# A Swin transformer block on one core: the order of its preparation, with weights loaded as two groups on two queues

## The chip, the core and the metric

The kernel runs on one core of a Trainium2 chip, all data in 32-bit floats. The metric is the device time of one execution in microseconds (us), the median of several runs.

## What is computed

The input x is 32 images of 56 x 56 positions with 128 channels, and the block is one shifted-window attention layer followed by a feed-forward layer:

```
h    = layernorm(x) * g1 + b1, rolled by (-3, -3), cut into 7 x 7 windows (49 tokens)
q,k,v = split(h @ w_qkv + b_qkv), 4 heads of 32 channels
attn = softmax(q k^T / sqrt(32) + rel_bias[head] + mask(-100 across a border))
x    = x + rolled back(attn v @ w_proj + b_proj)
out  = x + gelu((layernorm(x)*g2 + b2) @ w_fc1 + b_fc1) @ w_fc2 + b_fc2
```

## The kernel before, in words

The work is cut into **steps** of 14 image rows (two bands of 7 rows, 784 tokens), four to an image, 128 in all. A step's tokens lie as 7 tiles of 112 tokens x 128 channels. The instruction streams of the five engines are written out in full, without loops on the chip; `run_steps` (L61) calls each engine's `step(n)` for n from -3 to 129, and one `step(n)` holds pieces of several steps of data at once: statistics for step n+3 (VectorE, L638), normalising, transposing and the q product of step n+2, scores and attention of n+1, projection and the first layer of the feed-forward part of n, and so on. So the first three calls (n = -3, -2, -1) fill the pipeline. The order on each engine is fixed by hand, and semaphores join the engines.

**The start (the preparation).** SyncE issues the six transfers of the first step's tokens (`load(0, 0)`, L269), then thirteen transfers of weights, vectors and the mask (L270 to L277), all of which count up one semaphore, `weights_loaded`; then half of the relative-position table (`load_rel`, L254, seven transfers) and the tokens of steps 1 to 3. ScalarE's queue issues the other half of that table (L348). VectorE fills tiles with zeros (L482 to L490; the last is `psum`), waits for all thirteen transfers (L491), and folds the layernorm gains into the weights: `wqk`, `wv`, `wfc1` (L493 to L496). It splits `wqk` and `wfc1` into a rounded part `_hi` and a remainder `_lo` (L499 to L503), for products made as three passes in a faster format (`product`, L720).

TensorE waits for the same thirteen transfers (L667) and multiplies the weights by the layernorm offsets, three one-column products from `w_qkv` (L669) and four from `w_fc1` (L672). VectorE makes the biases from them (L508 to L512) and a widened copy of the v bias (L515), with which TensorE makes one more product (L676). From that VectorE makes `brow_proj` (L517), the row that is added to the tokens ahead of the projection's result. GpSimd waits for `weights_loaded` and `brow_ready` (L308, L309) before its first step, ScalarE for `weights_ready` and `bias_v_ready`.

**The first steps.** Only then do the steps begin. VectorE: `stats1(k)` (seven `bn_stats`, L532) and `mean_var` (six short operations, L539 to L548) for step 0, in call n = -3; the same for step 1, then `normalise` of step 0 (seven operations, L553), in call n = -2; statistics of step 2, `split_x` (L594, the remainder of band 1 of the transposed tokens) and `normalise` of step 1 in call n = -1; and in call 0 first `make_bias_rel` (four additions, L525: relative-position bias plus mask), then the scores of step 0 (L568 and on). GpSimd makes 1/sqrt(variance) with one power operation a step (`power`, L318) and adds `brow_proj` to the tokens (`add_row`, L321). TensorE transposes the seven normalised tiles (L695), ScalarE copies them out of PSUM (`copy_x`, L379) and rounds band 1 (L384). TensorE then makes q and k of band 0 (L728), q of band 1 when the split is there (L721 to L723), and the scores (L688).

Of the kernel before, what the change touches and what calls it, by code (L numbers as in the profile page):

```python
# [10 lines left out]
ALU = mybir.AluOpType  # L11
# [4 lines left out]
C = 128  # L16
# [31 lines left out]
def swin_block(nc, x, g1, b1, w_qkv, b_qkv, w_proj, b_proj, rel_slices, g2, b2, w_fc1, b_fc1, w_fc2,  # L48
# [4 lines left out]
    def has(k):  # L53

        return 0 <= k < steps

# [8 lines left out]
    with ExitStack() as ctx:  # L65
# [75 lines left out]
        weights_loaded = sem("weights_loaded")  # L141
# [7 lines left out]
        bias_v_ready = sem("bias_v_ready")  # L149
        brow_product = sem("brow_product")  # L150
# [109 lines left out]
        def _(sp):  # L260
# [9 lines left out]
            for dst, src in ((wqkv[:, :], w_qkv), (vecs[:, 0:1], g1), (vecs[:, 1:2], b1), (vecs[:, 2:3], g2),  # L270
                             (vecs[:, 3:4], b2), (bqkv[:, :], b_qkv), (wproj[:, :], w_proj),
                             (wfc1_raw[:, :], w_fc1), (bfc1[:, :], b_fc1),
                             (wfc2[:, :, :], w_fc2.rearrange("(k p) n -> p k n", p=C)),
                             (brow_proj_in[:, :], b_proj.to_broadcast([TOK, C])),
                             (brow_fc2[:, :], b_fc2.to_broadcast([TOK, C])),
                             (mask_sb[:, :, :, :], mask)):
                sp.dma_start(dst, src).then_inc(weights_loaded, 16)  # L277
# [23 lines left out]
        def _(pool):  # L301
# [6 lines left out]
            pool.wait_ge(weights_loaded, 13 * 16)  # L308
            pool.wait_ge(brow_ready, 1)  # L309
# [14 lines left out]
            def step(n):  # L324
# [16 lines left out]
                if has(n - 1):  # L341
                    wait(pool, var2_ready, upto(n - 1))
                    power(rstd2, ve2, rstd2_ready)
            run_steps(step)

        @block.scalar
        def _(act):
            load_rel(act, 1)  # L348
# [61 lines left out]
            def load_gelu_table():  # L410
                act.activation(table_probe[:, :], bias_h[:, 0:1], ACT.Gelu).then_inc(gelu_loaded, 1)
# [69 lines left out]
        def _(dve):  # L481
# [9 lines left out]
            dve.wait_ge(weights_loaded, 13 * 16)  # L491

            dve.tensor_scalar(wqk[:, 0, :], wqkv[:, 0:C], vecs[:, 0:1], SCALE, ALU.mult, ALU.mult)  # L493
            dve.tensor_scalar(wqk[:, 1, :], wqkv[:, C:2 * C], vecs[:, 0:1], None, ALU.mult)
            dve.tensor_scalar(wv[:, :], wqkv[:, 2 * C:3 * C], vecs[:, 0:1], None, ALU.mult)
            dve.tensor_scalar(wfc1[:, :], wfc1_raw[:, :], vecs[:, 2:3], None, ALU.mult).then_inc(weights_scaled, 1)  # L496

            dve.wait_ge(weights_scaled, 1)
            dve.tensor_copy(wqk_hi[:, :, :], wqk[:, :, :])  # L499
            dve.tensor_copy(wfc1_hi[:, :], wfc1[:, :]).then_inc(weights_scaled, 1)  # L500
            dve.wait_ge(weights_scaled, 2)
            dve.tensor_tensor(wqk_lo[:, :, :], wqk[:, :, :], wqk_hi[:, :, :], ALU.subtract)
            dve.tensor_tensor(wfc1_lo[:, :], wfc1[:, :], wfc1_hi[:, :], ALU.subtract).then_inc(weights_ready, 1)  # L503

            dve.wait_ge(bias_products, 1)
            made = psum[:, QKVO_BANK, :]
            for parity in range(2):
                dve.tensor_scalar(bias_q[:, parity:parity + 1], made[:, 0:1], bqkv[:, 0:1],  # L508
                                  parity_scale[:, parity:parity + 1], ALU.add, ALU.mult)
            dve.tensor_tensor(bias_k[:, :], made[:, 1:2], bqkv[:, 1:2], ALU.add)  # L510
            dve.tensor_tensor(bias_v[:, :], made[:, 2:3], bqkv[:, 2:3], ALU.add)
# [408 lines left out]
```

## Time and profile before

| | us |
|---|---|
| median of 3 runs | 3122.12 |
| lowest and highest run | 3111.51 and 3128.21 |
| profiled execution, own time | 3099.51 |
| its span, first to last instruction | 3097.7 |

In the profile, a row of the timeline gives the start, the duration, the engine, the source line, the operation with the tile written and the tiles read, the number of instructions merged into the row, and in brackets how long the engine had stood idle and what released it. PE is TensorE's matmul, PEld its weight load, DVE VectorE, ACT ScalarE, POOL GpSimd, SP SyncE; SPq and ACTq are the instructions by which a queue issues transfers. Over the whole span PE is busy for 97%, VectorE for 90%, ScalarE for 74% and GpSimd for 42%.

### The profile page before, as it was taken

Reading aid. Unit: us, or ns where it says so; the run is one execution under the profiler, and the core shown is the slowest. Engines: PE = TensorE matmul, PEld = TensorE weight load, DVE = VectorE, ACT = ScalarE, POOL = GpSimd, SP = SyncE. Lnnn points to the kernel's source line nnn. Section 1 sums busy time; section 2 is a strip of 40 time slices with the busy share of each in tenths; the row PEclk is TensorE's granted clock in tenths of the full one; section 3 lists DMA queues with packets and bytes.
Section 4 is the critical chain, followed back from the end, with each engine's and each line's share of the span. In section 5 each row is a group of like instructions: output and inputs, shape, how many; then the busy total and the mean of one; then the engine's idle time right before and its main releaser. Section 6 shows DMA issues by size and latency. Waiting matters only on the chain.

```text
span 3097.7 us, 119627 instructions
## 1 busy us (share of the span) xinstructions
PE 3003.0 (97%) x51984; PEld 2725.4 (88%) x51984; DVE 2803.2 (90%) x7463; ACT 2305.0 (74%) x4482; POOL 1306.6 (42%) x775
## 2 busy tenths in 40 slices
PE   5999999999999999999999999999999999999998
PEld 3898888989988898998899889988999888998897
DVE  7899988999989899999999999989999899999994
ACT  4777777777777777777777777777777777777774
POOL 2444444444434444444444444444444344444442
PEclk8999999999999999999999999999999999999999
DMA  1111111111111111111111111111111111111100
GB/s 55 34 34 34 44 34 34 33 44 34 34 33 44 34 34 35 43 34 33 44 33 34 40 37 34 36 41 34 34 39 39 33 34 39 39 33 37 41 18 22
DMA packets 217572, 111.81 MB, mean 36 GB/s; under 512 B 15094, under 2 KB 216790, under 8 KB 217046
## 3 DMA queue, kind: packets, MB, share of 16 engines
q1 hardware_dynamic: 216899, 104.14, 13.2%
q8 instruction: 408, 6.68, 0.9%
q14 instruction: 118, 0.97, 0.1%
q10 hardware_dynamic: 147, 0.02, 0.0%
HBM read 52.73 MB, written 51.38 MB: 34 GB/s over the span
## 4 chain that ended last, share of the span: by engine, by line
PE 59%; DVE 38%; issue 2%; ACT 0%; SPq 0%; DMA 0%; POOL 0%; POOLq 0%; ACTq 0%; DVEq 0%
PE psum L721 11%; DVE xn L553 9%; PE psum L722 7%; PE psum L723 7%; PE psum L688 7%; DVE row_sum L580 7%; PE psum L742 7%; PE psum L749 6%; PE psum L716 6%; DVE stream L587 4%; DVE scores L568 4%; DVE row_max L571 4%; DVE scores L573 4%; PE psum L703 4%; PE psum L695 3%; DVE x2T_lo L598 2%
## 5 line engine op out<-in xcount | busy, mean ns | idle before, releaser
L763 PEld LDWEIGHTS psum<-wfc,hT 128*112 128x112 f32 x7168 | 806.1, 177 | 39.2 <-issue 21.5
L763 PE MATMUL psum<-wfc,hT 128*112 128x128 f32 x7168 | 824.1, 273 | 1.5 <-ACT hT L407 1.5
L407 ACT ACTIVATE hT<-psum,bias_h 128x392 f32<-128x392 f32 x1024 | 578.8, 594 | 314.6 <-PE psum L723 301.7
L318 POOL TENSOR_TENSOR rstd<-ve,minus_half 112x7 f32<-112x7 f32 x256 | 381.1, 1489 | 986.7 <-DVE ve L548 986.7
L314 POOL TENSOR_TENSOR probs<-probs,row_inv 128x784 f32<-128x784 f32 x256 | 388.7, 1519 | 689.8 <-DVE row_inv L582 689.8
L553 DVE TENSOR_SCALAR xn<-stream,mean,rstd 112x128 f32<-112x128 f32 x896 | 460.4, 571 | 1.6 <-POOL rstd L318 1.6
L587 DVE TENSOR_TENSOR stream<-psum,stream 112x512 f32<-112x512 f32 (+1 forms) x512 | 305.6, 606 | 169.7 <-PE psum L749 153.0
L721 PE MATMUL psum<-x2T_hi,wfc_hi 128*128 128x392 f32 x1024 | 405.0, 395 | 9.2 <-DVE x2T_lo L598 2.0
L722 PE MATMUL psum<-x2T_hi,wfc_lo 128*128 128x392 f32 x1024 | 351.9, 344 | 12.4 <-issue 12.4
L723 PE MATMUL psum<-x2T_lo,wfc_hi 128*128 128x392 f32 x1024 | 351.9, 344 | 0.0
L394 ACT ACTIVATE qd<-psum,bias_q,parity_one 128x392 f32<-128x392 f32 x512 | 316.9, 669 | 3.3 <-PE psum L723 3.3
L321 POOL TENSOR_TENSOR stream<-stream,brow_fc 112x896 f32<-112x896 f32 x128 | 269.0, 2102 | 93.5 <-DVE xn L553 93.5
L721 PEld LDWEIGHTS psum<-x2T_hi,wfc_hi 128*128 128x128 f32 x1024 | 193.5, 189 | 106.5 <-DVE x2T_lo L598 87.4
L695 PE MATMUL psum<-ident,xn 112*128 112x112 f32 x1792 | 271.3, 268 | 10.6 <-DVE xn L553 9.1
L568 DVE TENSOR_TENSOR scores<-psum,bias_rel 128x784 f32<-128x784 f32 x256 | 247.2, 966 | 34.3 <-PE psum L688 34.2
L321 POOL TENSOR_TENSOR stream<-x_in,brow_proj 112x896 f32<-112x896 f32 x128 | 270.3, 2112 | 0.5 <-DMA out<-stream 0.5
L742 PE MATMUL psum<-wv,xT 128*113 128x128 f32 x2048 | 265.4, 272 | 0.0
L573 DVE TENSOR_TENSOR scores<-scores,row_max 128x784 f32<-128x784 f32 x256 | 249.5, 975 | 8.7
L571 DVE TENSOR_REDUCE row_max<-scores 128x16 f32<-128x784 f32 x256 | 248.3, 970 | 8.8
L353 ACT ACTIVATE probs<-scores 128x784 f32<-128x784 f32 x256 | 223.7, 874 | 42.5 <-DVE scores L573 41.1
L361 ACT ACTIVATE probsT<-psum 128x452 f32<-128x452 f32 x512 | 252.0, 550 | 0.6 <-PE psum L703 0.6
L389 ACT ACTIVATE x2T_hi<-psum 128x448 fp32r<-128x448 f32 (+1 forms) x256 | 127.5, 498 | 166.7 <-PE psum L695 166.6
(78 smaller groups left out, 5663.2 us busy)
## 6 DMA issues: line engine op xcount, KB each, us to landing
x_in<-in_x SPq DMA_DIRECT2D x224, 168.0 KB
out<-stream SPq DMA_DIRECT2D x224, 168.0 KB
x_in<-in_x SPq DMA_DIRECT2D x224, 17.5 KB
out<-stream SPq DMA_DIRECT2D x224, 17.5 KB
x_in<-in_x SPq DMA_DIRECT2D x224, 10.5 KB
out<-stream SPq DMA_DIRECT2D x224, 10.5 KB
x_in<-in_x SPq DMA_DIRECT2D x32, 96.0 KB
out<-stream SPq DMA_DIRECT2D x32, 96.0 KB
```

The costliest lines, as they stand in the source:

```text
L314: pool.tensor_tensor(p, p, r.unsqueeze(2).to_broadcast([128, 2 * WINDOWS, N]), ALU.mult).then_inc(probs_normed[band], 1)
L318: pool.tensor_tensor(rstd[:, :], ve[:, :], minus_half[:, :], ALU.pow).then_inc(ready, 1)
L321: pool.tensor_tensor(stream[:, k % STEPS, :, :], src[:, k % STEPS, :, :], row[:, :].unsqueeze(1).to_broadcast([TOK, TILES, C]), ALU.add).t ...
L407: act.activation(hT[:, chunk, band * BAND:(band + 1) * BAND], tok_psum(c)[:, 0:BAND], ACT.Gelu, bias=bias_h[:, chunk:chunk + 1]).then_inc( ...
L553: last = dve.tensor_scalar(dst[:, t, :], src[:, t, :], mean[:, t:t + 1], rstd[:, t:t + 1], ALU.subtract, ALU.mult)
L573: dve.tensor_tensor(rows, rows, mx.unsqueeze(2).to_broadcast([128, 2 * WINDOWS, N]), ALU.subtract).then_inc(scores_shifted[band], 1)
L587: dve.tensor_tensor(s, tok_psum(h)[0:TOK, 0:(t1 - t0) * C], s, ALU.add).then_inc(ready[h], 1)
L721: pe.matmul(made, w_hi, x_hi, start=True, stop=False)
L722: pe.matmul(made, w_lo, x_hi, start=False, stop=False)
L723: return pe.matmul(made, w_hi, x_lo, start=False, stop=True)
L742: last = pe.matmul(qkvo_psum(V_BANK[band])[0:rows, pair * C:(pair + 1) * C], windows[:, 0:rows], wv[:, :], start=True, stop=True)
L763: last = pe.matmul(tok_psum(h)[0:TOK, (t - t0) * C:(t - t0 + 1) * C], hT[:, chunk, t * TOK:(t + 1) * TOK], wfc2[:, chunk, :], start=chunk ...
```

## The change

The thirteen transfers become two groups. SyncE issues six (`front_loaded`): w_qkv, g1, b1, b_qkv, w_proj and b_proj. ScalarE's queue issues seven (`back_loaded`): g2, b2, w_fc1, b_fc1, w_fc2, b_fc2 and the mask, ahead of its half of the relative-position table. Statistics, power, normalising and transposing of step 0 move out of the step calls into the preparation: the statistics stand ahead of the wait for the front group, the normalising behind the scaling of `wqk` and `wv`, the transposes ahead of the wait for the back group. What belongs to `w_fc1` is prepared behind them. `fresh(k)` (0 < k < steps) takes the place of `has(k)` where step 0 has now been dealt with. TensorE waits for `weights_ready`, `bias_h_ready` and `brow_ready` before its first step call. GpSimd's power of step 0 stands ahead of its wait for the back group. The table-loading instruction of ScalarE reads `parity_one` in place of `bias_h`. No transfer and no arithmetic is added or removed.

```diff
+    def fresh(k):
+
+        return 0 < k < steps
...
 @block.sync
             load(0, 0)
-            for dst, src in ((wqkv[:, :], w_qkv), (vecs[:, 0:1], g1), (vecs[:, 1:2], b1), (vecs[:, 2:3], g2),
-                             (vecs[:, 3:4], b2), (bqkv[:, :], b_qkv), (wproj[:, :], w_proj),
...
-                sp.dma_start(dst, src).then_inc(weights_loaded, 16)
+            for dst, src in ((wqkv[:, :], w_qkv), (vecs[:, 0:1], g1), (vecs[:, 1:2], b1), (bqkv[:, :], b_qkv),
+                             (wproj[:, :], w_proj), (brow_proj_in[:, :], b_proj.to_broadcast([TOK, C]))):
+                sp.dma_start(dst, src).then_inc(front_loaded, 16)
             load_rel(sp, 0)
...
 @block.gpsimd
-            pool.wait_ge(weights_loaded, 13 * 16)
-            pool.wait_ge(brow_ready, 1)
...
-                if has(n + 2):
+                if fresh(n + 2):
                     wait(pool, var1_ready, upto(n + 2))
                     power(rstd1, ve1, rstd1_ready)
...
+            pool.wait_ge(var1_ready, 1)
+            power(rstd1, ve1, rstd1_ready)
+            pool.wait_ge(back_loaded, 7 * 16)
+            pool.wait_ge(brow_ready, 1)
             run_steps(step)
...
 @block.scalar
+            for dst, src in ((vecs[:, 2:3], g2), (vecs[:, 3:4], b2), (wfc1_raw[:, :], w_fc1), (bfc1[:, :], b_fc1),
+                             (wfc2[:, :, :], w_fc2.rearrange("(k p) n -> p k n", p=C)),
+                             (brow_fc2[:, :], b_fc2.to_broadcast([TOK, C])), (mask_sb[:, :, :, :], mask)):
+                act.dma_start(dst, src).then_inc(back_loaded, 16)
             load_rel(act, 1)
...
 @block.vector
-            dve.wait_ge(weights_loaded, 13 * 16)
...
+            dve.wait_ge(x_loaded[0], dma_count(0, 0))
+            stats1(0)
+            mean_var(raw1, part1, mean1, ve1, raw1_done, parts1_done, stats1_done, var1_ready, 1)
+
+            dve.wait_ge(front_loaded, 6 * 16)
+            dve.tensor_scalar(wqk[:, 0, :], wqkv[:, 0:C], vecs[:, 0:1], SCALE, ALU.mult, ALU.mult)
+            dve.tensor_scalar(wqk[:, 1, :], wqkv[:, C:2 * C], vecs[:, 0:1], None, ALU.mult)
+            dve.tensor_scalar(wv[:, :], wqkv[:, 2 * C:3 * C], vecs[:, 0:1], None, ALU.mult).then_inc(weights_scaled, 1)
+            dve.wait_ge(weights_scaled, 1)
+            dve.tensor_copy(wqk_hi[:, :, :], wqk[:, :, :]).then_inc(weights_scaled, 1)
+
+            dve.wait_ge(rstd1_ready, 1)
+            for h in range(2):
+                normalise(xn1, x_in[:, 0, :, :], mean1, rstd1, xn1_ready, h)
+
+            dve.wait_ge(weights_scaled, 2)
+            dve.tensor_tensor(wqk_lo[:, :, :], wqk[:, :, :], wqk_hi[:, :, :], ALU.subtract)
+            dve.wait_ge(bias_products, 1)
...
+            dve.wait_ge(back_loaded, 7 * 16)
+            dve.tensor_scalar(wfc1[:, :], wfc1_raw[:, :], vecs[:, 2:3], None, ALU.mult).then_inc(weights_scaled, 1)
+            dve.wait_ge(weights_scaled, 3)
+            dve.tensor_copy(wfc1_hi[:, :], wfc1[:, :]).then_inc(weights_scaled, 1)
+            dve.wait_ge(weights_scaled, 4)
+            dve.tensor_tensor(wfc1_lo[:, :], wfc1[:, :], wfc1_hi[:, :], ALU.subtract).then_inc(weights_ready, 1)
+            dve.wait_ge(bias_products, 2)
+            dve.tensor_tensor(bias_h[:, :], psum[:, QKVO_BANK + 1, 0:CHUNKS], bfc1[:, :], ALU.add).then_inc(bias_h_ready, 1)
+            dve.wait_ge(brow_product, 1)
+            dve.tensor_tensor(brow_proj[:, :], psum[0:TOK, QKVO_BANK, 0:C], brow_proj_in[:, :],
+                              ALU.add).then_inc(brow_ready, 1)
...
 @block.tensor
+            pe.wait_ge(front_loaded, 6 * 16)
+            for k in range(3):
+                last = pe.matmul(psum[:, QKVO_BANK, k:k + 1], wqkv[:, k * C:(k + 1) * C], vecs[:, 1:2],
+                                 start=True, stop=True)
+            last.then_inc(bias_products, 1)
+            pe.wait_ge(ident_ready, 1)
+            for h in range(2):
+                pe.wait_ge(xn1_ready[h], 1)
+                transpose_tiles(xn1, h, xT_made)
+            pe.wait_ge(back_loaded, 7 * 16)
+            for k in range(CHUNKS):
+                last = pe.matmul(psum[:, QKVO_BANK + 1, k:k + 1], wfc1_raw[:, k * C:(k + 1) * C], vecs[:, 3:4],
+                                 start=True, stop=True)
+            last.then_inc(bias_products, 1)
+            pe.wait_ge(bias_v_ready, 2)
+            pe.matmul(psum[0:TOK, QKVO_BANK, 0:C], bias_v_wide[:, :], wproj[:, :], start=True,
+                      stop=True).then_inc(brow_product, 1)
+            pe.wait_ge(weights_ready, 2)
+            pe.wait_ge(bias_h_ready, 1)
+            pe.wait_ge(brow_ready, 1)
```

## Rows read from the trace of the kernel before

**Rows 1.** The page: busy time of each engine.

```profile
PE 3003.0 (97%) x51984; PEld 2725.4 (88%) x51984; DVE 2803.2 (90%) x7463; ACT 2305.0 (74%) x4482; POOL 1306.6 (42%) x775
```

**Rows 2.** The timeline of SyncE's queue: each step's stores, from step 1 on.

```profile
118.05 2.26 SPq L267 DMA_DIRECT2D out<-stream  x6
...
141.33 2.26 SPq L267 DMA_DIRECT2D out<-stream  x6
...
167.46 3.35 SPq L267 DMA_DIRECT2D out<-stream  x9
...
2934.79 2.26 SPq L267 DMA_DIRECT2D out<-stream  x6
```

**Rows 3.** The waits of PE between 141 and 167 us (total, times, longest).

```profile
PE psum L716 <- issue: 2.6, 1, 2.6
```

**Rows 4.** The chain of waits in the first 120 us (start, duration, what).

```profile
8.71 4.91 DMA mask_sb<-in_mask
```

**Rows 5.** The timeline of SyncE's queue at the start.

```profile
0.74 2.20 SPq L263 DMA_DIRECT2D x_in<-in_x  x6
2.98 0.36 SPq L277 DMA_DIRECT2D wqkv<-in_w_qkv  x1
...
11.60 48.33 SPq L263 DMA_DIRECT2D x_in<-in_x  x39
```

**Rows 6.** The timeline of the engines during the preparation.

```profile
6.17 1.76 DVE L490 MEMSET psum<- 128x2048 f32 x1 [0.42 <-issue]
...
13.65 0.29 DVE L493 TENSOR_SCALAR wqk<-wqkv,vecs 128x128 f32<-128x128 f32 x1 [5.71 <-DMA mask_sb<-in_mask]
...
14.97 1.85 PE L672 MATMUL psum<-vecs,wfc_raw 128*128 128x1 f32 x8
...
15.76 0.68 DVE L503 TENSOR_TENSOR wfc_lo<-wfc,wfc_hi 128x512 fp32r<-128x512 f32 x1
...
17.82 0.77 PE L676 MATMUL psum<-wproj,bias_v_wide 128*112 128x128 f32 x2 [1.01 <-DVE bias_v_wide L515]
```

**Rows 7.** The same timeline, first steps: what the change moves, and what follows it.

```profile
18.84 1.44 DVE L532 BATCH_NORM_STATS2 raw<-x_in 112x6 f32<-112x128 f32 x7
...
21.37 1.49 POOL L318 TENSOR_TENSOR rstd<-ve,minus_half 112x7 f32<-112x7 f32 x1 [19.85 <-DVE ve L548]
22.90 1.89 DVE L553 TENSOR_SCALAR xn<-x_in,mean,rstd 112x128 f32<-112x128 f32 x7 [0.34 <-POOL rstd L318]
24.16 1.54 PE L695 MATMUL psum<-ident,xn 112*128 112x112 f32 x7 [5.57 <-DVE xn L553]
...
25.25 1.28 ACT L379 ACT_TABLE_LOAD   x1 [25.25 <-PE psum L695]
...
27.03 2.07 POOL L321 TENSOR_TENSOR stream<-x_in,brow_proj 112x896 f32<-112x896 f32 x1
...
27.62 2.98 PE L728 MATMUL psum<-xT,wqk 128*128 128x392 f32 x4 [1.92 <-ACT xT L379]
...
32.97 3.89 DVE L525 TENSOR_TENSOR bias_rel<-mask_sb,rel 128x392 f32<-128x392 f32 x4 [0.94 <-PE psum L688]
...
33.58 2.39 POOL L321 TENSOR_TENSOR stream<-x_in,brow_proj 112x896 f32<-112x896 f32 x1
```

**Rows 8.** Transfers of the first 70 us (KB, median us from issue to landing).

```profile
brow_proj_in<-in_b_proj SPq DMA_DIRECT2D x1, 56.0 KB, 3.7
```

**Rows 9.** Busy time by stretch: PE, PEld, DVE, ACT, POOL, then PEclk, DMA share, GB/s.

```profile
2.00:4.00 2.00, 0.00 (x0) 0.00 (x0) 1.62 (x2) 0.00 (x0) 0.00 (x0) 1.00 0.69 181
6.00:8.00 2.00, 0.00 (x0) 0.00 (x0) 1.76 (x1) 0.00 (x0) 0.00 (x0) 1.00 0.29 66
```

**Rows 10.** By tile or line: duration in ns as min/median/max, first and last start.

```profile
L525 DVE TENSOR_TENSOR bias_rel<-mask_sb,rel x4: 554/564/2453, 33.0 to 36.3; 128x392 f32<-128x392 f32 x4
...
L594 DVE TENSOR_TENSOR xT_lo<-xT,xT_hi x12: 556/556/1367, 28.2 to 289.9; 128x392 fp32r<-128x392 f32 x12
...
L553 DVE TENSOR_SCALAR xn<-stream,mean,rstd x4: 254/338/1589, 65.8 to 67.7; 112x128 f32<-112x128 f32 x4
```

More of the change, by code:

```diff
@@ L490, in _ @@
             dve.memset(psum[:, 0:4, :], 0.0).then_inc(weights_ready, 1)
-            dve.wait_ge(weights_loaded, 13 * 16)
[L493 to L511, printed above, removed]
-            dve.tensor_tensor(bias_h[:, :], made[:, 3:3 + CHUNKS], bfc1[:, :], ALU.add).then_inc(bias_v_ready, 1)
-            dve.wait_ge(bias_v_ready, 1)
-            dve.tensor_copy(bias_v_wide[:, :], bias_v[:, 0:1].to_broadcast([C, TOK])).then_inc(bias_v_ready, 1)
-            dve.wait_ge(brow_product, 1)
-            dve.tensor_tensor(brow_proj[:, :], psum[0:TOK, QKVO_BANK + 1, 0:C], brow_proj_in[:, :],
-                              ALU.add).then_inc(brow_ready, 1)
             def make_bias_rel():
                 dve.wait_ge(rel_loaded, 2 * WIN * 16)
+                dve.wait_ge(back_loaded, 7 * 16)
                 for last_band in range(2):
@@ new lines, in _ @@
+            dve.wait_ge(bias_products, 1)
+            made = psum[:, QKVO_BANK, :]
+            for parity in range(2):
+                dve.tensor_scalar(bias_q[:, parity:parity + 1], made[:, 0:1], bqkv[:, 0:1],
+                                  parity_scale[:, parity:parity + 1], ALU.add, ALU.mult)
+            dve.tensor_tensor(bias_k[:, :], made[:, 1:2], bqkv[:, 1:2], ALU.add)
+            dve.tensor_tensor(bias_v[:, :], made[:, 2:3], bqkv[:, 2:3], ALU.add).then_inc(bias_v_ready, 1)
+            dve.wait_ge(bias_v_ready, 1)
@@ L650, in step @@
                     split_x(n + 1, 1)
-                if has(n + 2):
+                if fresh(n + 2):
                     if n < 0:
@@ L655, in step @@
                     normalise(xn1, x_in[:, (n + 2) % STEPS, :, :], mean1, rstd1, xn1_ready, 1)
-                if has(n + 3):
+                if fresh(n + 3):
                     wait(dve, raw1_done, upto(n + 3))
@@ L665, in _ @@
         def _(pe):
-            pe.wait_ge(weights_loaded, 13 * 16)
-            for k in range(3):
-                pe.matmul(psum[:, QKVO_BANK, k:k + 1], wqkv[:, k * C:(k + 1) * C], vecs[:, 1:2],
-                          start=True, stop=True)
-            for k in range(CHUNKS):
-                last = pe.matmul(psum[:, QKVO_BANK, 3 + k:4 + k], wfc1_raw[:, k * C:(k + 1) * C], vecs[:, 3:4],
-                                 start=True, stop=True)
-            last.then_inc(bias_products, 1)
-            pe.wait_ge(bias_v_ready, 2)
-            pe.matmul(psum[0:TOK, QKVO_BANK + 1, 0:C], bias_v_wide[:, :], wproj[:, :], start=True,
-                      stop=True).then_inc(brow_product, 1)
-            pe.wait_ge(weights_ready, 2)
-            pe.wait_ge(ident_ready, 1)
             def make_scores(band):
@@ L797, in step @@
                     make_values(n + 1, 0)
-                if has(n + 2):
+                if fresh(n + 2):
                     wait(pe, gelu_done[4], upto(n - 1))
@@ L808, in step @@
                     make_scores(1)
-                if has(n + 2):
+                if fresh(n + 2):
                     wait(pe, gelu_done[3], upto(n - 1))
```

15 lines of the change are left out of this document (7 added, 8 removed).

## Prediction

> **What bounds the kernel now.** I began with the page: PE is busy for 97% of the span, VectorE for 90% [rows 1]. Busy shares are averages, so next the rhythm of the steps, read from SyncE's queue: consecutive stores start 23.28 us apart (141.33 - 118.05), and then once 26.13 us apart (167.46 - 141.33) [rows 2]. The ordinary step is TensorE's own length; in the long one PE stood for 2.6 us on "issue", that is with no other engine to wait for, in the middle of the small attention products of L716 [rows 3]. The change edits none of this. Its 128 steps come behind a start that it does edit, so I read the start as an offset: whatever the start gives, every later step is earlier by as much, as long as the filling of the pipeline is bound by a chain that begins there.
>
> The chain of waits of the first 120 us names that start: the mask, issued at 8.71 us, lands 4.91 us later and is the last of the thirteen transfers to arrive [rows 4]. SyncE issues one after another: tokens from 0.74, the first weight at 2.98, the tokens of steps 1 to 3 from 11.60, behind the mask [rows 5]. VectorE has finished its zero filling at 7.93 (6.17 + 1.76) and idles 5.71 us until 13.65 [rows 6]. Behind that lies a serial stretch: scaling, bias products and `brow_proj`, statistics of step 0 at 18.84, its power at 21.37, its seven normalising operations at 22.90, its transposes at 24.16 [rows 7]. The place to compare the two kernels is the end of `make_bias_rel`, 36.86 us (32.97 + 3.89) [rows 7]: behind it stands only VectorE's own work on the scores, which neither kernel can start sooner.
>
> **The change, step by step.** I lay the new order out with the old durations.
>
> 1. *Tokens of step 0.* VectorE may start their statistics at 7.93. From statistics to power takes 2.53 us (18.84 to 21.37), from power to normalising 1.53 (to 22.90), the seven operations 1.89 [rows 7]. So: power at 10.5, normalising 12.0 to 13.9. The transposes begin 1.26 us behind the first normalising operation (24.16 - 22.90) and take 1.54: 13.3 to 14.8. The scaling of `wqk`, `wv` and the rounding, some 1.0 us by the starts around L493, fit under the power's 1.5 us and cost nothing, if the front group has landed by about 11; without that cover they cost their own 1.0.
>
> 2. *The front group.* The issue of its last member moves forward: five issues at 0.47 us behind the one at 2.98 make 5.4. (0.47 is the spacing of the thirteen: 8.71 - 2.98 = 5.73 over twelve.) The slowest small one of its kind, `brow_proj_in`, took 3.7 us to land [rows 8]: 9.1. That leaves about 2 us of room before it is wanted.
>
> 3. *The back group.* Seven issues at 0.47 from about 0.8 put the mask at 3.6 and its landing, by its own 4.91, at 8.5. Both groups then want the transfer engines at once. The engines had room: 69% and 181 GB/s at 2 to 4 us, but 29% and 66 GB/s at 6 to 8, when SyncE was issuing small vectors [rows 9]. Tokens of step 0 and all thirteen are about 1.7 MB; at 181 GB/s from 2 us on that ends at 11.4. The group is first wanted by PE at 14.8. Nothing waits if it lands by then. At the worst, the engines do no better than the old start's mean, in which SyncE's pace was part: 1.7 MB from 2 to 13.6, 147 GB/s [rows 4]. SyncE now issues the tokens of steps 1 and 2 (0.8 MB) from 8.3 on, so these may all be carried as well before the group's last byte: 2.5 MB at 147 GB/s end at 19. I take 11.4, from the row of a stretch in which transfers were waiting, and keep 19 for the range.
>
> The Trainium skill (DMA: Bandwidth & Descriptors, "Issuing engines are not separate DMA queues") says that transfers started from several engines run on the same 16 DMA engines and interleave, and that one saves only the issuing time. By this the groups would land together, no later than the bytes allow, and the start keeps the sum below; the same rule says that tokens of step 0 can be held up by the back group, which is a rival below.
>
> 4. *Behind the transposes.* PE: four products with `w_fc1`, 1.85 us [rows 6], 14.8 to 16.7; then the product for `brow_proj`, from whose start to that of the statistics behind it pass 1.02 us (17.82 to 18.84) [rows 6, 7]. So statistics of step 1 start at 17.7. VectorE's work beside that ends sooner: behind 13.9 come `wqk_lo` and the biases (1.3 by the old starts), then scaling, rounding and remainder of `wfc1`, some 1.7 with its last piece 0.68 [rows 6]: 16.9. Here PE is the later by less than 1 us. ScalarE, released with the biases at 15.0, loads its table (1.28) [rows 7] and copies step 0 out by 17.3; before, this stood in the chain behind the transposes, now it is hidden beside the `w_fc1` work. GpSimd's and TensorE's waits for the back group hold nothing that is wanted earlier.
>
> 5. *The filling.* Statistics of step 1 at 17.7, its power 2.53 later at 20.2 to 21.7; statistics of step 2 (1.44) at 20.2 to 21.6. `split_x` no longer waits for ScalarE and runs 21.6 to 22.1 at its median of 0.56 [rows 10]. Before, it took 1.37, because GpSimd's `add_row` (27.03 to 29.10) [rows 7] was running. The same `add_row` now starts right behind the power, at 21.7, and falls on normalising of step 1. What this does is shown in a row of a later stage: under a long GpSimd operation one of four normalising operations takes 1589 ns where the others take 254 to 338 [rows 10]. So the first is held until about 23.9, and the seven end near 25.7. Of what was won on the split, 1.7 us go back. `mean_var` of step 2 (0.7) ends at 26.5, and `make_bias_rel` starts there. PE is not what it waits for: q and k take 2.98 from 17.9 [rows 7], q of band 1 starts behind the split at 22.1, and the scores follow about 2 us on.
>
> 6. *`make_bias_rel`.* Four at 0.56 [rows 10] from 26.5. GpSimd: power 26.5 to 28.0, `add_row` 28.0 to 30.1. Three pass, the fourth (28.2) is held until 30.1, as one was before (2453 ns against 564), and ends at 30.7.
>
> **The sum:** 36.86 - 30.7 = 6.2 us. The median of the runs is 3122.12, so I forecast **3115.9 us**. The profiled execution took 3099.51, 22.6 us less than that median and less than the lowest run shown; its successor should have a span near 3097.7 - 6.2 = 3091.5 if it were as lucky. That one gap is more than three times the gain. About 0.5% (15.6 us) is what a measurement here can tell from no change.
>
> Bounds of the gain: above, 9.7 us, the move of the first q product (27.62 to 17.9) [rows 7] if nothing collides. Below, 1.9: the back group at 19.1 holds PE up by 4.3 us (14.8 to 19.1), and 6.2 becomes 1.9.
>
> **The rivals.**
>
> *The gain is held whole.* GpSimd's `add_row` slips between VectorE's work and all of it goes through: up to 9.7 us, 3112.4. For it: VectorE's order against GpSimd's is decided here by tenths. Against: twice in the old start, and in the row of a later stage, one was held.
>
> *The wait comes back as another.* Sharing delays the tokens of step 0, the front or the back group until 15 us or later. The gain is 0 to 3, the time 3119 to 3122. For it: both queues ask at once for what one spread over 8.7 us, and the mask alone took 4.91 [rows 4]. Against: the engines' 29% share while SyncE issued small vectors [rows 9].
>
> *Slower: the pauses of PE move.* About every fifth gap between stores is longer than 23.3 us, some 27 from the one at 167.46 to the one at 2934.79 [rows 2]. The one at 167.46 is 2.85 us over, with PE's pause on L716 in it [rows 3]. The change puts some three more waits into PE's stream ahead of the first step, which moves the place of every later pause. If five more of the 27 fell on L716, at 2.8 us each instead of an estimated 0.5 elsewhere, 11.5 us are added, 6.2 are won, and the time is 3127. It decides from three on (6.9 against 6.2). Against: three instructions are little beside the some 400 matmuls of a step, of which L716 has 128, so at most one pause should change its place.
>
> *The change doesn't do what it says.* If the code order on VectorE let the front group's wait come first, step 0 would gain nothing; the diff shows statistics ahead of it, so I hold this at nothing and count it under the second rival.
>
> **How the numbers follow.** The forecast's case (a gain of 3 to 8): 0.65. The whole gain: 0.12. The wait comes back: 0.15. PE's pauses, or anything else that makes it slower: 0.08. None but a part of the last can by itself reach 15.6 us; what can is the scatter of the runs, 16.7 us from lowest to highest and 28.7 with the profiled one. Around a gain of 6, a difference of medians with a spread of some 8 us passes 15.6 about one time in eight, and the whole gain adds a little: faster 0.16, slower 0.04, same 0.80. The range: down to 3101, the whole gain and 11 us of scatter (3122.12 - 3111.51); up to 3128, the slower rival, which is also the highest run.
>
> **What would show it.** In the changed kernel's profile: statistics of step 0 within 0.5 us of 7.9; normalising from 12.0; VectorE's wait for the front group under the power; PE's `w_fc1` products right behind the transposes with no transfer as releaser; the first q product near 18; the first normalising operation of step 1 near 2 us long; the end of `make_bias_rel` near 30.7; stores 23.3 us apart as before, the first one 6 us sooner. I am wrong if PE or VectorE stands on a transfer at 11 to 15 us, if the lead at `make_bias_rel` is not there at the first store, or if the pauses at L716 become more.

## The result and the profile after

| | before | after |
|---|---|---|
| median of 11 runs, us | 3117.28 | 3131.86 |
| lowest and highest, us | 3101.30, 3128.21 | 3125.10, 3143.53 |
| profiled execution, own time, us | 3099.51 | 3132.80 |
| its span, us | 3097.7 | 3131.1 |

The ratio of the times is **1.0054** with a 95% interval of 1.0031 to 1.0077: the changed kernel is slower, by about 17 us (the means of the runs; the medians differ by 14.6), a small change but one that the interval keeps apart from none. Its median of 3131.86 lies above the predicted range. Yet its start went as planned, and better. The timeline of the changed kernel's start, to hold against [rows 6] and [rows 7]:

```profile
7.85 1.39 DVE L511 BATCH_NORM_STATS2 raw<-x_in 112x6 f32<-112x128 f32 x7
...
11.06 0.29 DVE L585 TENSOR_SCALAR wqk<-wqkv,vecs 128x128 f32<-128x128 f32 x1 [0.99 <-DMA brow_proj_in<-in_b_proj]
...
11.98 1.88 DVE L532 TENSOR_SCALAR xn<-x_in,mean,rstd 112x128 f32<-112x128 f32 x7
...
13.24 1.54 PE L699 MATMUL psum<-ident,xn 112*128 112x112 f32 x7 [0.72 <-DVE xn L532]
...
14.57 1.73 PE L783 MATMUL psum<-vecs,wfc_raw 128*128 128x1 f32 x8
...
17.16 1.44 DVE L511 BATCH_NORM_STATS2 raw<-x_in 112x6 f32<-112x128 f32 x7
...
17.50 2.95 PE L732 MATMUL psum<-xT,wqk 128*128 128x392 f32 x4 [0.58 <-DVE brow_proj L616]
...
21.14 2.15 POOL L320 TENSOR_TENSOR stream<-x_in,brow_proj 112x896 f32<-112x896 f32 x1
21.26 3.65 DVE L532 TENSOR_SCALAR xn<-x_in,mean,rstd 112x128 f32<-112x128 f32 x7
...
25.57 2.00 DVE L504 TENSOR_TENSOR bias_rel<-mask_sb,rel 128x392 f32<-128x392 f32 x4
```

`make_bias_rel` ends at 27.57 instead of 36.86 us, 9.3 us sooner. In these two traces the lead is still whole at the first store. SyncE's queue, kernel before:

```profile
94.75 2.27 SPq L267 DMA_DIRECT2D out<-stream  x6
```

and the changed kernel:

```profile
85.45 2.28 SPq L273 DMA_DIRECT2D out<-stream  x6
...
108.75 2.25 SPq L273 DMA_DIRECT2D out<-stream  x6
```

94.75 - 85.45 = 9.3 us, and the next step again takes 23.30. What costs comes later and a little at a time. I took the 121 gaps between consecutive stores in each trace and added up what each has over 23.3 us: 44.5 us in the kernel before, 86.0 in the changed one, 41.5 more. With the start (-9.3) and the last stretch (+1.5, from the last of those stores to the end) that is, to within 0.3 us, the 33.4 us between the two spans. The waits of PE say what the long gaps are made of; "issue" is time in which PE waits for no other engine and no transfer of data. Kernel before (total, times, longest):

```profile
PE psum L716 <- issue: 19.2, 9, 3.0
...
PE psum L722 <- issue: 12.4, 8, 1.7
...
PE psum L749 <- issue: 1.8, 6, 0.4
```

Changed kernel:

```profile
PE psum L720 <- issue: 37.1, 16, 3.0
PE psum L725 <- issue: 14.8, 8, 2.3
...
PE psum L753 <- issue: 4.0, 8, 0.9
```

L716 and L720 are the same code, the small products of the attention, 128 matmul records a step. TensorE paused there 16 times instead of 9. **One such pause, step by step.** The same step of both kernels, PE's timeline of the kernel before:

```profile
788.70 1.37 PE L716 MATMUL psum<-probsT,vs 49*32 49x49 f32 x128
```

and of the changed kernel:

```profile
780.50 1.25 PE L720 MATMUL psum<-probsT,vs 49*32 49x49 f32 x115
784.70 0.41 PE L720 MATMUL psum<-probsT,vs 49*32 49x49 f32 x13 [2.95 <-issue]
785.04 0.69 PE L725 MATMUL psum<-x2T_hi,wfc_hi 128*128 128x392 f32 x1
```

115 records run, PE stands for 2.95 us, and the other 13 follow. The clock falls as well. The changed kernel by stretches (columns as in [rows 9]):

```profile
785.00:788.00 3.00, 3.00 (x19) 2.96 (x10) 0.00 (x0) 2.21 (x6) 2.57 (x2) 0.50 0.03 5
788.00:791.00 3.00, 3.00 (x28) 2.85 (x29) 0.73 (x2) 1.25 (x2) 0.00 (x0) 0.61 0.00 0
791.00:795.00 4.00, 4.00 (x84) 3.94 (x81) 3.90 (x11) 2.42 (x5) 0.00 (x0) 1.00 0.02 4
```

The granted clock is at half, 1.2 GHz, behind the pause, and back at 2.4 GHz by 791. So a pause of 2.95 us made a gap of 28.89 us between stores, 5.6 us over. Such half-clock stretches between 100 and 3050 us: 5, of 20 us together, in the kernel before, 15, of 68 us together, in the changed one. Every one of these 20 begins during or just behind a pause of PE on "issue".

**Why at 115.** PE's instructions come in pages: the profile counts 408 transfers of 6.68 MB on the instruction queue q8, that is 16.4 KB each, and TensorE has 51,984 weight loads, 51,984 matmuls and 520 semaphore instructions in the record, 104,488, or 256.1 a page. I counted the weight loads, matmuls and semaphore instructions of TensorE that had started ahead of each pause. In all fourteen kernels whose step has TensorE's 816 instructions (the two here and e1 to e10, e13 and e14 below) every pause on "issue" of over 1.2 us in the steady part, 249 of them, lies at the same remainder of that count modulo 256: where a new page begins. The Trainium skill (Runtime: NRT & Kernel Launch, "Instruction fetch mechanics") has the same page, 16 KiB or 256 instructions, and calls the cost of crossing into one mostly hidden. The trace agrees on the size. On the cost it does not agree in the attention products and just behind them: there 128 records, 256 instructions, pass in 1.37 us, and from the start of a page's transfer to the first instruction of that page pass 2.2 to 3.1 us when TensorE has to wait for it. The pauses of over 1.2 us at L722 and L725 lie 4 or 5 matmuls behind the attention products. Pages that begin elsewhere in the step brought no such pause in these two traces.

When its transfer starts decides. The transfers in the 2 us ahead of the step's attention products, kernel before, from 786.5 to 788.5:

```profile
q8 instruction: 1, 0.02, 3.8%
```

In the changed kernel the same stretch (778.3 to 780.5) shows no transfer on q8; it comes behind, between 780.5 and 784.7:

```profile
q8 instruction: 1, 0.02, 1.5%
```

The same holds for every page that begins in the last 17 of the attention products (place 111 or later) from the fourth step on, 236 in the fourteen traces. In 158 cases its transfer started 0.86 to 2.1 us behind the first attention product, and TensorE paused for 1.9 to 3.2 us. In 16 it started between 0.13 and 1.2 us ahead of it, and TensorE paused for 0.4 to 1.0 us. In the other 62 it started about 1 us ahead or more, with a pause under 0.3 us or none.

The change adds two semaphore instructions to TensorE's stream (522 for 520) ahead of the first step, from its waits for `weights_ready`, `bias_h_ready`, `brow_ready` and `ident_ready`. So each page begins two instructions, one matmul, earlier in the program: at matmul 115 of the attention products in place of 116, at 123 in place of 124. ("At 115" means that 115 of the 128 matmuls run ahead of the pause.) A step has 816 instructions; 816 and 256 share the divisor 16, so over 16 steps pages begin at 51 places of a step, 16 instructions apart, and only the count modulo 16 matters.

### The profile page after: what moved, and what is told of

Its sections match the earlier page's. It is cut to its first block, busy times and chain, and to the rows that moved or that the text cites. A ratio compares the mean times of both kernels' runs of the same rounds, so it can differ in the third digit from the quotient of the medians.

```text
span 3131.1 us, 119628 instructions
## 1 busy us (share of the span) xinstructions
PE 3025.1 (97%) x51984; PEld 2748.8 (88%) x51984; DVE 2801.9 (89%) x7463; ACT 2309.0 (74%) x4482; POOL 1307.9 (42%) x775
## 3 DMA queue, kind: packets, MB, share of 16 engines
q8 instruction: 408, 6.68, 0.9%
## 4 chain that ended last, share of the span: by engine, by line
PE 59%; DVE 37%; issue 3%; ACT 0%; SPq 0%; DMA 0%; POOL 0%; DVEq 0%
PE psum L725 11%; DVE xn L532 9%; PE psum L727 7%; PE psum L726 7%; DVE row_sum L559 7%; PE psum L692 7%; PE psum L746 7%; PE psum L753 7%; PE psum L720 6%; DVE stream L566 4%; DVE scores L547 4%; DVE row_max L550 4%; DVE scores L552 4%; PE psum L707 4%; PE psum L699 3%
## 5 line engine op out<-in xcount | busy, mean ns | idle before, releaser
L725 PE MATMUL psum<-x2T_hi,wfc_hi 128*128 128x392 f32 x1024 | 409.3, 400 | 23.9 <-issue 14.8
L725 PEld LDWEIGHTS psum<-x2T_hi,wfc_hi 128*128 128x128 f32 x1024 | 195.4, 191 | 123.3 <-DVE x2T_lo L577 87.3
L707 PE MATMUL psum<-ident,probs 113*128 113x113 f32 x2048 | 249.6, 265 | 2.3 <-POOL probs L313 2.3
```

Of the source, the lines that this page charges most:

```text
L725: pe.matmul(made, w_hi, x_hi, start=True, stop=False)
```

## The experiments

Two theories stand against each other. **PLACE**: the pauses come from where the pages begin. **START**: the earlier start, or the second queue, brings them by itself (other timing against transfers, another clock). All ratios are to the kernel before.

**e1, the changed kernel with the pages of the kernel before.** 14 semaphore instructions more make 16 with the change's two. Two waits share one instruction, so 28 waits, all met at once and standing where TensorE is idle until 11 us:

```diff
+            for _ in range(28):
+                pe.wait_ge(ident_ready, 1)
             pe.wait_ge(front_loaded, 6 * 16)
```

> The changed kernel with 14 semaphore instructions more at the very start of TensorE's stream, where it is idle until 11 us. Their waits are met at once. Together with the 2 that the change added, every page of 256 instructions begins 16 instructions earlier in the program than in the kernel before; a step has 816 instructions, 816 and 256 have 16 as greatest common divisor, so the places in a step at which pages begin are those of the kernel before again. Theory PLACE (where pages begin in the attention products sets how often TensorE pauses there): pauses as in the kernel before (17 of over 1.2 us, some 33 us in all, against 22), the start's lead of 9.3 us stays, so 3105 to 3112, ratio 0.996 to 0.999. Theory START (the earlier or differently loaded start itself brings the pauses, by its timing against the transfers or the clock): pauses and time as in the changed kernel, 3125 to 3140, ratio near 1.005.

Measured: 3101.28 us, ratio **0.9942** (0.9919 to 0.9966), a little better than the 0.996 to 0.999 expected. Its waits of PE:

```profile
PE psum L720 <- issue: 22.5, 11, 2.9
PE psum L726 <- issue: 9.7, 8, 1.9
```

Faster than both kernels, by adding instructions that do nothing: the changed kernel's start and its second queue are in it, its extra pauses are not. START falls.

**e2, the kernel before with the pages of the changed one.** Two semaphore instructions, in TensorE's first idle stretch:

```diff
+            for _ in range(4):
+                pe.wait_ge(ident_ready, 1)
             pe.wait_ge(weights_loaded, 13 * 16)
```

> The kernel before with 2 semaphore instructions more at the start of TensorE's stream, in its idle time, nothing else. Theory PLACE: the pauses of the changed kernel without its lead: some 22 over 1.2 us, 3137 to 3145, ratio 1.007 to 1.010. Theory START: as the kernel before, ratio 1.000.

Measured: 3143.43 us, ratio **1.0069** (1.0046 to 1.0092).

```profile
PE psum L718 <- issue: 38.4, 15, 2.9
PE psum L723 <- issue: 14.6, 8, 2.0
```

Two instructions in an idle stretch cost 21 us. PLACE gave it, with 1.007 to 1.010.

**e3, eight more** instructions in the changed kernel, at e1's place:

```diff
+            for _ in range(16):
+                pe.wait_ge(ident_ready, 1)
             pe.wait_ge(front_loaded, 6 * 16)
```

> The changed kernel with 8 semaphore instructions more: pages begin 10 instructions earlier than in the kernel before. Theory PLACE: a third pattern of pauses, other places in the step; the time differs from both kernels by some us, in a direction that it does not give. Theory START: as the changed kernel, near 1.005.

Measured: 3114.83 us, ratio 0.9998 (0.9982 to 1.0014): a third pattern (below).

**e4, the second queue alone.** The kernel before, with the seven transfers of the back group issued by ScalarE's queue, all thirteen still on one semaphore:

```diff
-            for dst, src in (...):
-                sp.dma_start(dst, src).then_inc(weights_loaded, 16)
+            for dst, src in ((wqkv[:, :], w_qkv), ...):
+                sp.dma_start(dst, src).then_inc(weights_loaded, 16)
...
+            for dst, src in ((vecs[:, 2:3], g2), ...):
+                act.dma_start(dst, src).then_inc(weights_loaded, 16)
```

> The kernel before with seven of the thirteen transfers issued by ScalarE's queue, everything else waiting for all thirteen as before, TensorE's stream unchanged. The last weight was in at 13.65 us; with both queues at once I expect 11 to 11.5, so a lead of 2 to 2.7 us at every later point and no change in the pauses: ratio 0.999. If two queues bring the pauses (theory START in its queue form), ratio 1.004 to 1.008.

Measured: 3111.83 us, ratio 0.9993 (0.9975 to 1.0012). VectorE starts on the weights at

```profile
12.05 0.29 DVE L492 TENSOR_SCALAR wqk<-wqkv,vecs 128x128 f32<-128x128 f32 x1 [4.12 <-DMA brow_proj_in<-in_b_proj]
```

1.6 us sooner than at 13.65, less than the 2 to 2.7 expected; the attention pauses stay as in the kernel before (10, 23.1 us). The start's gain is too small for the interval to show, and in the trace it doesn't last: 1.8 us are left at the end of `make_bias_rel`, and the first store, at 96.03, is 1.3 us later than the kernel before's. Between these two points this trace has 27 us at half clock, that of the kernel before 20. The queue brings no pauses.

**e5, e6, e7: other places.** 4, 6 and 12 instructions more in place of the 14 of e1, each in its own kernel:

```diff
+            for _ in range(8):
+                pe.wait_ge(ident_ready, 1)
             pe.wait_ge(front_loaded, 6 * 16)
```

with `range(12)` in e6 and `range(24)` in e7.

> The changed kernel with 4 semaphore instructions more at the start of TensorE's stream. In the attention products, 128 matmuls a step, pages then begin at every eighth matmul up to number 113 and 121 (kernel before: 116 and 124, the changed kernel: 115 and 123). Over the six traces so far, pages that begin at 115, 119, 123, 124 or 127 brought a pause of 2.3 to 3.2 us in most cases, at 116 in one of seven, at 111 and lower in none. Theory WINDOW (any place from about 112 on but 116 pauses, each with the same chance): two such places here, a time between e3 and the changed kernel, ratio 1.000 to 1.005, unless 113 is still free of them: then one place, ratio 0.992 to 0.995. Theory START: 1.005.

> The same with 6 more: pages begin at 112 and 120. Theory WINDOW: one or two places as for e5; if 112 is free, ratio 0.992 to 0.995, 15 to 25 us under the kernel before. Theory START: 1.005.

> The same with 12 more: pages begin at 117 and 125. Theory WINDOW: two places, 12 to 14 long pauses, ratio 1.000 to 1.005. If the rare pauses at 116 are the beginning of a quiet stretch, 117 is quiet too and the ratio is 0.993 to 0.996. Theory START: 1.005.

Measured: e5 1.0059 (1.0037 to 1.0081), e6 0.9996 (0.9970 to 1.0023), e7 1.0031 (1.0006 to 1.0056). The first is above the 1.000 to 1.005 of its expectation. The trace shows the place itself, PE's timeline of e5:

```profile
403.31 1.24 PE L720 MATMUL psum<-probsT,vs 49*32 49x49 f32 x113
407.16 0.32 PE L720 MATMUL psum<-probsT,vs 49*32 49x49 f32 x15 [2.62 <-issue]
```

113 by the count of the instructions, 113 in the trace. WINDOW, as these expectations put it, failed: 113 and 117 paused every time, while 112 never did, and e6 with its single place at 120 did not reach 0.995 because the next page, just behind the attention products, became dear:

```profile
PE psum L720 <- issue: 22.7, 9, 3.2
PE psum L725 <- issue: 20.6, 8, 3.2
```

**e8, the new order on one queue.** The back group issued by SyncE behind the front group, with e1's 14 instructions:

```diff
+            for dst, src in ((vecs[:, 2:3], g2), ...):
+                sp.dma_start(dst, src).then_inc(back_loaded, 16)
...
-                act.dma_start(dst, src).then_inc(back_loaded, 16)
...
+            for _ in range(28):
+                pe.wait_ge(ident_ready, 1)
             pe.wait_ge(front_loaded, 6 * 16)
```

> The changed kernel's order, with all thirteen transfers issued by SyncE again (front group first, then back group, two semaphores), and the 14 semaphore instructions of e1, so that pages begin where they do in e1. If the new order gives the whole lead and the second queue nothing: front group in at 9 to 9.5 us, back group at 13.7, before the transposes end (14.4), lead 9 us as in e1, ratio 0.992 to 0.997. If the second queue is part of the lead: the back group is late and the lead falls to 6 or less, ratio 0.996 to 0.999.

Measured: 3095.06 us, ratio **0.9916** (0.9890 to 0.9943). The lead is e1's without the second queue (9.4 us at the end of `make_bias_rel`, 9.2 in e1); TensorE has its front group at 8.32 us instead of 11.08:

```profile
8.32 1.41 PE L776 MATMUL psum<-vecs,wqkv 128*128 128x1 f32 x6 [8.32 <-DMA brow_proj_in<-in_b_proj]
...
14.44 1.73 PE L785 MATMUL psum<-vecs,wfc_raw 128*128 128x1 f32 x8
```

and its `w_fc1` products wait for no transfer. The second queue is worth nothing here.

**e9 and e10, the same without padding.** e9 takes the change's two semaphore instructions out, with all of these lines; e10 takes out only one, with the last two removed lines alone:

```diff
             for k in range(3):
+                if k == 1:
+                    pe.wait_ge(ident_ready, 1)
...
-            pe.wait_ge(ident_ready, 1)
...
-            pe.wait_ge(weights_ready, 2)
-            pe.wait_ge(bias_h_ready, 1)
             pe.wait_ge(brow_ready, 1)
```

> The changed kernel without its two separate semaphore instructions: TensorE waits for brow_ready alone before its first step (VectorE makes it behind weights_ready and bias_h_ready), and its wait for ident_ready stands ahead of the second of the three bias products. No padding. By the program's list pages begin at matmuls 116 and 124 again. Theory PLACE: as e1, 6 to 8 long pauses in the attention products, ratio 0.991 to 0.997, faster than both kernels. Theory START: 1.005.

> The same, with the wait for ident_ready left where the change has it: one semaphore instruction more than the kernel before. A page then begins between the weight load and the product of matmul 115, so the next whole matmul is 116. Theory PLACE gives one of its neighbours: 1.005 as the changed kernel if the place of the weight load counts, 0.992 to 0.997 as e1 if that of the product does. Theory START: 1.005.

Measured: e9 3106.04 us, 0.9972 (0.9942 to 1.0002), e10 3129.35 us, 1.0051 (1.0027 to 1.0075). e10 behaves as the changed kernel: it paused at its first place in all seven such steps. PE's weight loads there, in the one such step in which the kernel before paused too:

```profile
406.55 1.17 PEld L716 LDWEIGHTS psum<-probsT,vs 49*32 49x32 f32 x117 [0.33 <-issue]
410.81 0.21 PEld L716 LDWEIGHTS psum<-probsT,vs 49*32 49x32 f32 x11 [3.10 <-issue]
```

and in e10:

```profile
399.53 1.16 PEld L720 LDWEIGHTS psum<-probsT,vs 49*32 49x32 f32 x116 [0.33 <-issue]
403.42 0.17 PEld L720 LDWEIGHTS psum<-probsT,vs 49*32 49x32 f32 x12 [2.72 <-issue]
```

Both run 116 products ahead of the pause. In the kernel before the weight load of the next one has run too, in e10 it hasn't. So a page begins with that product in the kernel before and with its weight load in e10, half a matmul later than the expectation puts it. The same product pauses, and one instruction decides whether it does so rarely or every time. e9's median is 7.5 us under that of the kernel before on the same chip (3113.52), its interval just touches 1.

**e11 and e12, another length of step.** 16 semaphore instructions more in each step of the changed kernel, and 40 (e11) or 24 (e12) at e1's place, which set where the pages begin.

```diff
                 if has(n - 1):
+                    for _ in range(32):
+                        pe.wait_ge(ident_ready, 1)
                     wait(pe, xT_copied[0], upto(n + 2))
...
+            for _ in range(80):
+                pe.wait_ge(ident_ready, 1)
             pe.wait_ge(front_loaded, 6 * 16)
```

(`range(48)` in e12).

> The changed kernel with 16 semaphore instructions more in each step of TensorE, ahead of the second feed-forward product of half 0 (waits met at once), and 40 at its start. A step then has 832 instructions, whose greatest common divisor with 256 is 64: pages begin at 13 places of a step instead of 51, in the attention products at matmuls 15, 47, 79 and 111 and next 15 matmuls behind their end, none of which paused long in any trace. Theory PLACE: no long pause is left; the 40 to 50 us by which gaps between stores exceeded 23.3 us fall to under 10, against the cost of 2048 semaphore instructions: nothing if TensorE's sequencer runs ahead there, 0.05 us each if not (100 us). Ratio 0.980 to 0.985 in the first case, up to 1.02 in the second. Theory START: no page matters, ratio 1.005 plus that cost.

> The same with 24 in place of 40 at the start: pages begin at matmuls 23, 55, 87 and 119, every fourth step at 119, where e3 paused in six of seven. Theory PLACE: some 26 of 31 such steps pause for 2.8 us and lose 4 to 5 us each, 105 to 130 us over e11 (ratio 3 to 4 percent above it). Theory START: as e11.

Measured: e11 3273.78 us, 1.0515 (1.0456 to 1.0575), e12 3266.99 us, 1.0491 (1.0435 to 1.0546). The ratios expected for PLACE failed, e11's 0.980 to 1.02 and e12's 3 to 4 percent above e11. The instructions are not free in the middle of a step: an ordinary gap between stores of e11 is

```profile
489.96 2.27 SPq L273 DMA_DIRECT2D out<-stream  x6
514.15 2.25 SPq L273 DMA_DIRECT2D out<-stream  x6
538.32 2.25 SPq L273 DMA_DIRECT2D out<-stream  x6
```

24.17 us, 0.87 over 23.30, or 54 ns for each of the 16: 111 us of the 160 by which e11 is slower than the kernel before. And place 111 was not quiet:

```profile
PE psum L767 <- issue: 129.0, 126, 1.6
PE psum L720 <- issue: 66.2, 27, 2.9
```

In the 816-instruction step a page beginning at 111 never paused (e3, seven such steps); in this one it did in 25 of 31. In e12 place 119 paused in 26 of 31, as expected. So the number of the matmul is not the cause by itself. Something else in the step counts too; the 16 instructions stand ahead of the attention products, but how they do it is not shown.

**e13, sixteen more.** If the count modulo 16 is what matters, this is the changed kernel again.

```diff
+            for _ in range(32):
+                pe.wait_ge(ident_ready, 1)
             pe.wait_ge(front_loaded, 6 * 16)
```

> The changed kernel with 16 semaphore instructions more at the start of TensorE's stream. By the program's list pages begin at matmuls 115 and 123 of the attention products again, as without them, in other steps. Theory PLACE: the period is 16, so this is the changed kernel's time again, ratio 1.003 to 1.008, pauses at 115 in all of seven or eight. If what made e1 fast was the added instructions or their time, and not their number modulo 16, it is as e1, 0.992 to 0.997.

Measured: 3133.57 us, ratio **1.0062** (1.0043 to 1.0081), with a pause at 115 in all of eight steps; attention pauses

```profile
PE psum L720 <- issue: 42.0, 17, 3.1
```

**e14, new order, one queue, no padding.** e8's move of the seven transfers with all of e9's lines, and no `range` of waits:

```diff
-                act.dma_start(dst, src).then_inc(back_loaded, 16)
+                sp.dma_start(dst, src).then_inc(back_loaded, 16)
...
-            pe.wait_ge(weights_ready, 2)
-            pe.wait_ge(bias_h_ready, 1)
             pe.wait_ge(brow_ready, 1)
```

> The changed order with the two separate semaphore instructions taken out as in e9, and all transfers on SyncE as in e8; no padding. Pages begin at 116 and 124. Theory PLACE, and the second queue worth nothing: as e8 and e9, ratio 0.991 to 0.998. If e8 was faster than e1 because of the single queue, it is under e9's 0.997, near 0.992.

Measured: 3106.46 us, ratio **0.9968** (0.9947 to 0.9989): faster than both kernels, without padding. It is like e9 and not like e8's 0.9916.

All kernels of the 816-instruction step together. "Shift" is how many instructions TensorE's stream has more than the kernel before's; pauses are those of the attention products in the profiled execution, the lead is how much earlier than in the kernel before its first store was issued.

| kernel | shift, and modulo 16 | pages begin at (of 128) | pauses, us | lead, us | ratio |
|---|---|---|---|---|---|
| before | 0 | 116, 124 | 9, 19.2 | 0 | 1 |
| e4 | 0 | 116, 124 | 10, 23.1 | -1.3 | 0.9993 |
| e9 | 0 | 116, 124 | 12, 26.2 | 9.0 | 0.9972 |
| e14 | 0 | 116, 124 | 11, 21.9 | 7.1 | 0.9968 |
| e1 | 16, 0 | 116, 124 | 11, 22.5 | 6.5 | 0.9942 |
| e8 | 16, 0 | 116, 124 | 11, 21.8 | 8.2 | 0.9916 |
| e10 | 1 | 116, 124, each with its weight load | 14, 32.2 | 6.4 | 1.0051 |
| after | 2 | 115, 123 | 16, 37.1 | 9.3 | 1.0054 |
| e2 | 2 | 115, 123 | 15, 38.4 | -0.4 | 1.0069 |
| e13 | 18, 2 | 115, 123 | 17, 42.0 | 7.5 | 1.0062 |
| e5 | 6 | 113, 121 | 16, 41.3 | 8.3 | 1.0059 |
| e6 | 8 | 112, 120 | 9, 22.7 | 9.1 | 0.9996 |
| e3 | 10 | 111, 119, 127 | 12, 28.9 | 8.0 | 0.9998 |
| e7 | 14 | 117, 125 | 16, 38.9 | 8.3 | 1.0031 |

Over the six traces of shift 0, a page that began at 116 brought a pause of over 1.2 us in 6 of 44 steps; at 115, over the three of shift 2, it did in 22 of 22. The later places differ less: 38 of 48 at 124, 20 of 24 at 123.

The six traces of shift 0 have 44.5 to 63.9 us of gaps over 23.3 us, 54 on average; the three of shift 2 have 74.3, 86.0 and 86.0, 82 on average. 28 us more, less the lead of 9.3, is 19 us, against the 17 us of the measured ratio. The profiled execution of the kernel before was simply a lucky one: 44.5 is the least of the six. Each trace is a single execution and not always one near its kernel's median: e5's and e8's were the slowest of their runs, e3's and e10's the fastest.

## Why the prediction was wrong

*What bounds the kernel* was right, and it held the reason for the miss. A start is an offset only if the steps behind it stay as they are. I wrote that the change edits none of this, the steps' code; it edits where that code lies in the pages.

*Parts 1 to 3, the start.* Statistics at 7.85 (predicted 7.93), normalising at 11.98 (12.0), transposes at 13.24 (13.3), `w_fc1` products at 14.57 (14.8), with no transfer as releaser. The front group landed at 11.06, not 9.1: two us late, but within the cover of the power, so it cost at most 0.2 us (the power ended at 11.78). On one queue, in e8, the group was there by 8.32. The back group did not hold anything up, as forecast. Its last transfer, the mask, was issued at 3.77 and took 6.0 us:

```profile
mask_sb<-in_mask ACTq DMA_DIRECT2D x1, 392.0 KB, 6.0
```

That is 9.8 us, later than the 8.5 of its own 4.91, earlier than the 11.4 taken for the group, and ahead of the front group's 11.06.

*Parts 4 to 6, the filling.* Statistics of step 1 at 17.16 (17.7). The collision with GpSimd's `add_row` was there: the first normalising operation of step 1 took 2114 ns (predicted near 2 us), the seven ended at 24.91 (25.7). The group of those seven by tile, with the shortest, middle and longest duration:

```profile
L532 DVE TENSOR_SCALAR xn<-x_in,mean,rstd x7: 334/336/2114, 21.3 to 24.6; 112x128 f32<-112x128 f32 x7
```

The term that was mis-sized is the last: no operation of `make_bias_rel` was held. It ran 2.00 us in one piece from 25.57 and was over at 27.57, just as `add_row` began at 27.47. The 0.9 us won ahead of it carried it past the collision, and the sum became 9.3 instead of 6.2 us.

*The lead stays.* Right in this trace: 9.3 us at the first store. It is in part luck: in the ten other kernels with the new order and a step of 816 instructions the lead was 8.9 to 9.5 us at the end of `make_bias_rel` and 6.4 to 9.1 at the first store.

*The step that failed* is the third rival, "the pauses of PE move", which got 0.08. That added waits move the pauses, the sign and the line L716 were right. That the pauses lie where pages begin it did not have, and its size was wrong: I argued that "three instructions are little beside the some 400 matmuls of a step" and that "at most one pause should change its place". The change moved **every** page, by one matmul, and those at two places matter. At 116, one page in seven brought a pause in the kernel before; at 115, seven in seven did in the changed one. I had taken a pause as a thing that either falls on L716 or does not, when two neighbouring matmuls of L716 have such different odds. The price of 2.8 us was also low: with the half clock behind it a pause costs up to 5.9 us (the longest gap is 29.21 us). A count of PE's instructions from one pause to the next (often 4096, sixteen pages, and always whole pages) was to be had from the trace before, and it would have shown that each pause lies at a page's beginning.

*The other rivals.* "The gain is held whole" (0.12) came true for the start, 9.3 of at most 9.7, and not for the time. "The wait comes back as another" did not: e4, e8 and the changed kernel show no wait on a transfer that costs.

*The range* took the slower case at 3127 with five pauses moved. The measured 3131.86 goes with seven more attention pauses in the profiled executions, each dearer than assumed. The forecast's base was itself high: 3122.12 was the median of three runs, that of eleven is 3117.28. Against this lower base the miss is larger, a loss of about 17 us where a gain of 6.2 was forecast.

## What stays open

Why a page's transfer starts ahead of the attention products in one kernel and only about when TensorE runs dry in another is not shown. In the fourteen traces none started between 0.13 us ahead of the first attention product and 0.86 us behind it. The choice varies from step to step with odds that go with the place (at 124 in the kernel before, five of eight; at 115, every time), and e11 shows that the place inside the attention products alone doesn't set them. Whether e8's 0.9916 is truly better than e14's 0.9968 is also open. Their intervals just part, they ran on different chips, and their pages begin at the same matmuls, in other steps. e1 stands to e9 in the same way (0.9942 and 0.9972, intervals that overlap). Whether the 14 added instructions or the steps on which the pages fall are worth something of themselves, no run separates.

## What to carry to other kernels

In a fully written-out kernel bound by TensorE, a change of a few instructions anywhere ahead of the steady part shifts all its instruction pages, and that can outweigh what the change is for: count TensorE's instructions before and after, semaphore instructions included. Where a small change has an effect that its own stretch of the trace doesn't show, pad the stream in an idle stretch so that the count modulo the period (here 16) is the old one, and measure again; e1 and e2 told the two causes apart in one go. To move work into an idle start is worth about what it seemed: 9.3 us in the changed kernel's trace, 6.4 to 9.1 in the others, and a ratio of 0.9968 in e14, which needs neither padding nor a second queue.

## What was not expected of the hardware

- Two semaphore instructions in TensorE's idle start cost 0.69% (e2, 21 us), and fourteen in the changed kernel won 1.1% (1.0054 to 0.9942).
- A half-clock stretch behind a pause is not rare: in the fourteen traces there are 157 between 100 and 3050 us, and each begins during or shortly behind a pause on "issue" of about 1.4 us or more.
- In the middle of a step a semaphore instruction whose wait is already met cost 54 ns of TensorE's time (e11).
- With two queues issuing at once, one issue of SyncE's took 1.63 us (`wproj`; 1.07 to 1.80 in e1, e4 and e9), against 0.43 in the kernel before and in e8 and e14, and the front group landed 2.7 us later than from one queue (11.06 against 8.32). The changed kernel's SyncE queue:

```profile
4.81 1.63 SPq L278 DMA_DIRECT2D wproj<-in_w_proj  x1
...
6.48 0.43 SPq L278 DMA_DIRECT2D brow_proj_in<-in_b_proj  x1
```
